# Attention scores of two heads in one matmul over all 128 rows, in a gated cross-attention and FFN kernel

## The chip, the cores and the metric

The kernel runs on one core of a Trainium2 chip. The metric is the device time of one execution in microseconds (us); lower is better. The core's engines are named as the profile names them: PE is the matmul engine (TensorE) and PEld its weight loads, DVE is VectorE, ACT is ScalarE, POOL is GpSimd, and SP is the engine from whose queue almost all transfers are issued.

## What is computed

```python
def reference(x, ctx_1024, g_xattn, g_ffn, ...):
    def xattn(q, k, v, Wq, Wk, Wv, Wo, bo):            # 16 heads of 16 dimensions
        qh = einsum('bse,hed->bhsd', q, Wq); kh = ... ; vh = ...
        scores = einsum('bhsd,bhtd->bhst', qh, kh) / sqrt(16)
        scores = where(causal, scores, -1e9)
        out = einsum('bhst,bhtd->bhsd', softmax(scores), vh)
        return concat(out) @ Wo.T + bo
    def ffn(x, ...):                                   # 256 -> 1024 -> 1024 -> 1024 -> 256
        h = silu(tlin(x, w1)) * tlin(x, w2)
        h = gelu(tlin(h, h1)); h = gelu(tlin(h, h2))
        return tlin(h, w3)                             # ternary weights, one scale per output
    x = x + tanh(g_xattn) * xattn(layernorm(x), ctx, ctx, ...)
    return x + tanh(g_ffn) * ffn(layernorm(x), ...)
```

`x` and `ctx_1024` are 64 x 128 x 256 in float32, so every one of the 64 batch rows is a sequence of 128 positions.

## The kernel before

The 64 batch rows are worked off in 32 blocks of two rows each. While the attention of block n runs, the FFN of block n-1 runs beside it, and the first steps of the attention of block n+1 are taken at the end. The order is written out by hand as one list of steps for a whole block, `ORDER` (lines 40 to 50), and one for the first block, `PROLOGUE` (lines 33 to 39). Every engine walks the same list and takes the steps that concern it, in that order; a step with a plus sign belongs to the next block. Semaphores hold an engine that comes too early. An engine's queue is strictly in order, so an instruction that waits holds all behind it.

The steps by name. On PE: `S` scores, `PV` probabilities times values, `Q`, `K`, `V` projections, `To` and `X2` transposes, `O` output projection, `L1` to `L4` the FFN layers (8 steps each for L1, L2 and L3, 4 for L4). On DVE: `s` scales and masks one group of four heads (one PSUM bank of scores), `m` its maximum and exp bias, `nh` normalises, `g` and `f` the two halves of the SiLU product of an L1 step, `b2` and `b3` sum an FFN step's two halves, `w3` takes low parts, `o` the residual and the statistics, `n2` the second layer norm, `x2` splits the transposed result into high and low parts, `y` scales the FFN's output. On ACT: `e` exponentials, `a1` the tanh of an L1 step, `h`, `a2`, `a3` copies and gelus, `to`, `x2`. On POOL: `p` splits probabilities into two fp16 parts, `nm`, `l`, `w2`, `n2`, `rx`, `z`. On SP: `D` transposes probabilities by DMA, `qw` and `kw` write the split queries and keys to DRAM, `qr.0`, `qr.1`, `kr.0`, `kr.1` bring them back for batch row 0 or 1 of the block, `lc`, `lt`, `lx`, `lr` are loads, `mv` a move and `sy` the store.

**Precision and layout of the scores.** Queries and keys are split into a high and a low part in fp32r. `place_parts` (line 340) lays them out for the score matmuls: a head's 16 dimensions times 4 combinations of parts (`COPIES = 4`, four transfers of 128 KB for each of q and k and each batch row) fill 64 partitions, so `q4` and `k4` hold two heads one above the other in the two halves of the 128 partitions.

**The scores.** `scores(n, u)` (line 921) has 4 steps per block, `S.0` to `S.3`. One step gives two groups of four heads, that is both score banks: 8 matmuls, in 4 pairs. In a pair one matmul uses the upper 64 rows and bank 0, the other the lower 64 rows and bank 1; each streams 128 key columns against 128 query columns as weights. A step waits until both banks were read by `s`. FFN matmuls use all 128 rows.

**FFN banks.** Three PSUM banks rotate over the FFN steps. `L1.3` needs the bank of `L1.0`, which is free once `f.0` is done. `L4.0` waits for the sums `b3.6` and `b3.7` (before_ffn, line 283). `L1.0` waits for `x2.1` of DVE.

Of the kernel before, what the change touches and what calls it, by code (L numbers as in the profile page):

```python
# [27 lines left out]
def steps(text):  # L28
# [5 lines left out]
    q.0 K qw Q.0 lc+ Q.1 k st v q.1 k+ W.0 kw W.1 s.0 s.1 V m.0 e.0 p.0 s.2 K+ W.2 S.0 Q.0+ m.1 lx+ p.1 qr.0 kr.0  # L34
    lt+ S.1 e.1 p.2 Q.1+ m.2 s.3 e.2 W.3 S.2 m.3 S.3 p.3 qr.1 s.4 PV.0 s.5 PV.1 m.4 PV.2 p.4 q.0+ q.1+ s.6 e.3 e.4
    kr.1 PV.3 W.4 m.5 m.6 e.5 p.5 nh.0 nm.0 s.7 W.5 D.0 D.1 kw+ nh.1 nm.1 To.0 PV.4 m.7 p.6 W.6 rx e.6 e.7 W.7 D.2
    st+ nh.2 O.0 p.7 V+ PV.5 lr PV.6 o.0 D.3 D.4 PV.7 D.5 n2.0 nm.2 to.0 nm.3 W.8 D.6 W.9 W.10 nh.3 v+ to.1 To.1 D.7
    qw+ O.1 kr.0+ F.0 F.1 o.1 x2.0 qr.0+ n2.1 s.0+ s.1+ X2.0 x2.1 rx+ p.0+ qr.1+ S.0+ X2.1 lr+ m.0+ s.2+ kr.1+ m.1+
""")
ORDER = steps("""  # L40
    lc+ S.1 L1.0 L1.1 lt+ sy L1.2 e.0 S.2 a1.0 s.3 e.1 a1.1 L1.3 h.0 L1.4 L1.5 l.0 L1.6 L1.7 a1.2 g.0 K+ a1.3 p.1
    PV.0 l.1 h.1 h.2 PV.1 L2.0 l.2 l.3 l.4 a1.4 a1.5 f.0 h.3 L2.1 g.1 f.1 h.4 l.5 l.6 g.2 l.7 a1.6 f.2 g.3 L2.2 f.3
    g.4 L2.3 f.4 L2.4 g.5 f.5 L2.5 g.6 f.6 L2.6 g.7 L2.7 h.5 a1.7 h.6 h.7 p.2 f.7 D.0 e.2 s.4 PV.2 D.1 p.3 PV.3 m.2
    m.3 m.4 b2.0 e.3 S.3 Q.0+ mv nh.0 kw+ b2.1 w2.0 L3.0 L3.1 D.2 k+ e.4 s.5 b2.2 b2.3 w2.1 w2.2 D.3 m.5 D.4 lx+
    b2.4 Q.1+ b2.5 a2.0 a2.1 a2.2 w2.3 w2.4 w2.5 L3.2 L3.3 To.0 PV.4 a2.3 b2.6 p.4 a2.4 a2.5 w2.6 PV.5 a2.6 a2.7
    L3.4 L3.5 b2.7 nm.0 s.6 s.7 O.0 w2.7 L3.6 PV.6 p.5 m.6 PV.7 V+ b3.0 To.1 L3.7 nh.1 m.7 p.6 O.1 b3.1 nm.1 e.5
    b3.2 e.6 e.7 D.5 p.7 q.0+ q.1+ a3.0 b3.3 S.0+ qw+ st+ w3.0 nm.2 to.0 X2.0 a3.1 a3.2 w3.1 a3.3 b3.4 b3.5 nh.2 o.0
    L4.0 a3.4 nh.3 D.6 L4.1 a3.5 b3.6 n2.0 nm.3 D.7 w3.2 v+ b3.7 o.1 s.0+ n2.1 kr.0+ rx+ m.0+ p.0+ w3.3 to.1 qr.0+
    a3.6 x2.0 a3.7 lr+ kr.1+ X2.1 s.1+ x2.1 m.1+ qr.1+ L4.2 z.0 L4.3 y.0 s.2+ z.1 y.1
# [1059 lines left out]
```

## Time and profile before

| | us |
|---|---|
| median of 3 runs | 1824.99 |
| lowest and highest run | 1816.38, 1828.99 |
| the profiled execution | 1814.27 |
| its span, from first to last instruction | 1812.5 |
| mean granted PE clock, share of full speed | 0.98 |
| PE busy | 1743.9 (96%) |
| DVE, ACT, POOL busy | 1383.7, 1222.9, 1081.5 |

The profile comes from one execution. The span is divided by engine and line; matmuls are pipelined, so their durations overlap, and what a matmul costs in a stream is the distance from its start to the next one's, not its own duration. The first 93 us are the prologue with the first block's attention, then 31 blocks follow that are alike, and the last stretch is the FFN of the last block alone.

### The profile page before, as it was taken

Reading aid. Unit: us, or ns where it says so; the run is one execution under the profiler, and the core shown is the slowest. Engines: PE = TensorE matmul, PEld = TensorE weight load, DVE = VectorE, ACT = ScalarE, POOL = GpSimd, SP = SyncE. Lnnn points to the kernel's source line nnn. Section 1 sums busy time; section 2 is a strip of 40 time slices with the busy share of each in tenths; the row PEclk is TensorE's granted clock in tenths of the full one; section 3 lists DMA queues with packets and bytes.
Section 4 is the critical chain, followed back from the end, with each engine's and each line's share of the span. In section 5 each row is a group of like instructions: output and inputs, shape, how many; then the busy total and the mean of one; then the engine's idle time right before and its main releaser. Section 6 shows DMA issues by size and latency. Waiting matters only on the chain.

```text
span 1812.5 us, 40485 instructions
## 1 busy us (share of the span) xinstructions
PE 1743.9 (96%) x11526; PEld 1481.4 (82%) x11526; DVE 1383.7 (76%) x3059; ACT 1222.9 (67%) x2952; POOL 1081.5 (60%) x1388
## 2 busy tenths in 40 slices
PE   4399999999999999999999999999999999999998
PEld 2288888888888888888888888888888888888876
DVE  4777887777787777787777888777788777788764
ACT  3476666677676677676767666667666667767664
POOL 2466566566656566666566665556656556665652
PEclk7599999999999999999999999999999999999999
DMA  7744545444445444454444454444454544445520
GB/s 278 227 107 121 140 127 138 112 127 115 133 136 138 114 127 115 129 142 130 120 117 126 123 139 127 132 111 127 119 136 127 140 113 126 113 133 141 126 46 8
DMA packets 395547, 231.38 MB, mean 128 GB/s; under 512 B 283136, under 2 KB 373504, under 8 KB 393984
## 3 DMA queue, kind: packets, MB, share of 16 engines
q1 hardware_dynamic: 393360, 219.23, 46.0%
q10 hardware_dynamic: 2160, 11.81, 1.8%
q8 instruction: 13, 0.21, 0.0%
q14 instruction: 14, 0.11, 0.0%
HBM read 113.53 MB, written 41.94 MB: 86 GB/s over the span
## 4 chain that ended last, share of the span: by engine, by line
PE 92%; DMA 2%; issue 2%; DVE 1%; POOL 1%; ACT 1%; SPq 0%; POOLq 0%; ACTq 0%; DVEq 0%
PE ffn L957 70%; PE work L894 13%; PE s_bank L931 4%; PE pv L948 3%; PE work L1037 2%; DMA pT<-p_parts 2%; DMA aw<-in_attn_w 0%; DVE wlow L669 0%; POOL p_parts L452 0%; SPq L348 0%; POOL p_parts L454 0%; DMA cT<-in_ctx_T 0%; ACT probs L799 0%; POOL heads L464 0%; DVE probs L594 0%
## 5 line engine op out<-in xcount | busy, mean ns | idle before, releaser
L636 DVE TENSOR_REDUCE full<-ffn 128x256 f32<-128x512 f32 x512 | 352.5, 689 | 261.1 <-PE ffn L957 259.1
L957 PE MATMUL ffn<-hb,W 128*128 128x512 f32 x2048 | 518.2, 403 | 1.0 <-POOL hb L491 1.0
L957 PE MATMUL ffn<-ha,W 128*128 128x512 f32 x2048 | 477.9, 393 | 0.6 <-POOL ha L486 0.6
L957 PEld LDWEIGHTS ffn<-ha,W 128*128 128x128 f32 x2048 | 382.1, 188 | 83.5 <-POOL ha L486 1.7
L957 PEld LDWEIGHTS ffn<-hb,W 128*128 128x128 f32 x2048 | 380.1, 188 | 79.1 <-POOL hb L491 1.6
L799 ACT ACTIVATE probs<-probs,exp_bias 128x128 f32<-128x128 f32 x1024 | 320.3, 390 | 70.7 <-DVE exp_bias L604 69.8
L454 POOL TENSOR_TENSOR p_parts<-probs,p_parts 128x512 f16<-128x512 f32 x256 | 299.5, 1170 | 20.5
L452 POOL CAST p_parts<-probs 128x512 f16<-128x512 f32 x256 | 162.3, 634 | 216.3 <-ACT probs L799 172.0
L817 ACT ACTIVATE full<-full,cols 128x256 f32<-128x256 f32 x512 | 253.8, 496 | 0.0
L957 PE MATMUL ffn<-x2T_hi,W 128*128 128x256 f32 x1024 | 252.2, 287 | 0.0
L491 POOL TENSOR_TENSOR hb<-full,hb 128x256 fp32r<-128x256 f32 x256 | 189.5, 740 | 99.6 <-ACT full L817 91.9
L957 PE MATMUL ffn<-x2T_lo,W 128*128 128x256 f32 x1024 | 245.3, 280 | 0.0
L816 ACT ACTIVATE hb<-full,cols 128x256 fp32r<-128x256 f32 x256 | 129.1, 504 | 100.6 <-DVE full L636 99.1
L957 PEld LDWEIGHTS ffn<-x2T_hi,W 128*128 128x128 f32 x1024 | 193.2, 189 | 4.4
L594 DVE SCALAR_TENSOR_TENSOR probs<-s_bank,rstd,causal 128x512 f32<-128x512 f32 x256 | 187.6, 744 | 11.7 <-PE s_bank L931 8.3
L486 POOL TENSOR_TENSOR ha<-full,ha 128x256 fp32r<-128x256 f32 x256 | 184.2, 739 | 15.5 <-ACT ha L831 12.0
L957 PEld LDWEIGHTS ffn<-x2T_lo,W 128*128 128x128 f32 x1024 | 193.3, 189 | 0.0
L840 ACT ACTIVATE full<-ffn,half_s 128x256 f32<-128x256 f32 x256 | 119.4, 466 | 84.2 <-PE ffn L957 58.9
L602 DVE TENSOR_REDUCE negmax<-probs 128x4 f32<-128x512 f32 x256 | 173.5, 678 | 0.0
L816 ACT ACTIVATE ha<-full,cols 128x256 fp32r<-128x256 f32 x256 | 128.5, 502 | 51.6 <-DVE full L636 51.2
L957 PE MATMUL ffn<-W,ha 128*128 128x256 f32 x1024 | 143.2, 288 | 1.0 <-DVE full L636 0.9
L957 PEld LDWEIGHTS ffn<-W,ha 128*128 128x128 f32 x1024 | 126.3, 189 | 7.1 <-DVE ha L642 5.7
(80 smaller groups left out, 2273.9 us busy)
## 6 DMA issues: line engine op xcount, KB each, us to landing
q<-q_saved SPq DMA_DIRECT2D x256, 128.0 KB, 2.7
k<-k_saved SPq DMA_DIRECT2D x256, 128.0 KB, 2.8
q_saved<-q_parts SPq DMA_DIRECT2D x32, 512.0 KB, 2.9
k_saved<-k_parts SPq DMA_DIRECT2D x32, 512.0 KB, 3.0
wnat<-in_ffn_w ACTq DMA_DIRECT2D x11, 1024.0 KB, 6.6
xT<-in_x_T SPq DMA_DIRECT2D x32, 256.0 KB, 2.8
cT<-in_ctx_T SPq DMA_DIRECT2D x32, 256.0 KB, 2.8
x_in<-in_x SPq DMA_DIRECT2D x32, 256.0 KB, 2.8
```

Source lines behind the costliest of these rows:

```text
L452: pool.tensor_copy(p_parts[:, t % 2, 0], probs[:, t % PSLOTS]).then_inc(p_hi_ready, 1)
L454: pool.tensor_tensor(p_parts[:, t % 2, 1], probs[:, t % PSLOTS], p_parts[:, t % 2, 0], ALU.subtract)\
L486: pool.tensor_tensor(ha_lo[:, k], full[:, k % 4], ha_hi[:, k], ALU.subtract)\
L491: pool.tensor_tensor(hb_lo[:, k], full[:, k % 4], hb_hi[:, k], ALU.subtract)\
L594: dve.scalar_tensor_tensor(probs[:, slot], s_bank[t % SBANKS][:].rearrange("p (h t) -> p h t", h=4), rstd[:, t // QROW:t // QROW + 1], cau ...
L602: dve.tensor_reduce(negmax[:, slot], probs[:, slot], AX_X, ALU.max, negate=True).then_inc(max_ready, 1)
L636: dve.tensor_reduce(full[:, m % 4], src[:].rearrange("p (a t) -> p t a", a=2), AX_X, ALU.add).then_inc(done, 1)
L799: last = act.activation(probs[:, slot, h], probs[:, slot, h], ACT.Exp, bias=exp_bias[:, slot, h:h + 1])
L816: act.activation(hi[:, m], f, ACT.Gelu, scale=scales[:, m:m + 1]).then_inc(hi_sem, 1)
L817: act.activation(f, f, ACT.Gelu, scale=scales[:, m:m + 1]).then_inc(hi_sem, 1)
L894: last = pe.matmul(dst, lhsT(kt), rhs(kt), start=kt == 0, stop=kt == KE - 1)
L957: return pe.matmul(dst, w, h, **flags)
```

## The change

The keys of a pair of heads are laid out in two blocks of columns: `k4` gets a dimension `e` of size 2, with the keys of the upper head in columns e=0 of partitions 0 to 63, those of the lower head in columns e=1 of partitions 64 to 127, and zeros elsewhere. One POOL memset at the start writes the zeros. One matmul over all 128 rows with 256 key columns then gives the scores of both heads. A score step now makes one group of four heads (one bank, two matmuls of 256 columns), so there are 8 steps per block, `S.0` to `S.7`; step t waits for the mask of group t-2. The permutation of the heads in the weights, made on the host, changes with it. `k4` takes twice the room. Each k transfer of 128 KB becomes two of 64 KB, so `kr` issues 8 transfers instead of 4; `qr` stays. Both lists of steps are new. For the stretch around the end of a block they read, per engine:

```
PE  before  L3.7 O.1 S.0+ X2.0 L4.0 L4.1 X2.1 L4.2 L4.3 | S.1 L1.0 L1.1 L1.2 S.2 L1.3 ...
PE  after   L3.7 O.1 L4.0 S.0+ L4.1 X2.0 L4.2 X2.1 L4.3 | S.1 S.2 L1.0 S.3 L1.1 L1.2 S.4 L1.3 ...
DVE before  b3.7 o.1 s.0+ n2.1 m.0+ w3.3 x2.0 s.1+ x2.1 m.1+ y.0 s.2+ y.1 | s.3 g.0 f.0 g.1 ...
DVE after   b3.7 o.1 s.0+ n2.1 w3.3 m.0+ x2.0 x2.1 y.0 s.1+ m.1+ y.1 | g.0 s.2 f.0 g.1 ...
SP  before  D.5 qw+ D.6 D.7 kr.0+ qr.0+ lr+ kr.1+ qr.1+ | lc+ lt+ sy D.0
SP  after   D.5 sy qw+ D.6 D.7 kr.0+ qr.0+ qr.1+ lr+ | kr.1 lc+ lx+ D.0
```

Elsewhere in the block, `S.5` stands after `L1.7`, `S.6` between the two `Q` steps and `S.7` between `L3.0` and `L3.1`; `q.0+` and `q.1+` of DVE stand before `b3.1` instead of after `b3.2`.

```diff
-        k4 = sb("k4", [P, ROWS, QROW, KE, P], F32R)
+        k4 = sb("k4", [P, ROWS, QROW, 2, KE, P], F32R)
...
+                if kind == "kr" and isinstance(n, int) and n == 0 and row == 0:
+                    sp.wait_ge(keys_cleared, 1)
...
                 for copy in range(COPIES):
-                    part = copy % 2 if kind == "qr" else copy // 2
-                    sp.dma_start(dst[copy:P:COPIES, row].rearrange("p j m t -> p j (m t)").bitcast(F32),
-                                 saved[:, part, row].rearrange("(p j) x -> p j x", j=QROW))\
-                        .then_inc(q_placed[row] if kind == "qr" else k_placed[row], 16)
+                    if kind == "qr":
+                        sp.dma_start(q4[copy:P:COPIES, row].rearrange("p j m t -> p j (m t)").bitcast(F32),
+                                     q_saved[:, copy % 2, row].rearrange("(p j) x -> p j x", j=QROW))\
+                            .then_inc(q_placed[row], 16)
+                    else:
+                        for e in range(2):
+                            sp.dma_start(k4[e * HALF + copy:(e + 1) * HALF:COPIES, row, :, e]
+                                         .rearrange("p j m t -> p j (m t)").bitcast(F32),
+                                         k_saved[e * HALF:(e + 1) * HALF, copy // 2, row]
+                                         .rearrange("(p j) x -> p j x", j=QROW)).then_inc(k_placed[row], 16)
...
             pool.memset(vs[:], 1.0).then_inc(pool_const, 1)
+            pool.memset(k4[:].bitcast(F32), 0.0).then_inc(keys_cleared, 1)
...
-            def scores(n, u):
-
-                row = u // 2
-                wait(pe, masked_ready, n * NQ + 2 * u)
-                if u % 2 == 0:
+            def scores(n, t):
+
+                row, j = t // QROW, t % QROW
+                wait(pe, masked_ready, n * NQ + t - 1)
+                if j == 0:
                     wait(pe, q_placed[row], 16 * COPIES * (n + 1))
-                    wait(pe, k_placed[row], 16 * COPIES * (n + 1))
-                for i in range(4):
-                    j, m = u % 2 * 2 + i // 2, i % 2
-                    for e in range(2):
-                        last = pe.matmul(s_bank[e][:, i * P:(i + 1) * P], q4[e * HALF:(e + 1) * HALF, row, j, m],
-                                         k4[e * HALF:(e + 1) * HALF, row, j, m], start=True, stop=True)
-                        if i == 3:
-                            last.then_inc(scores_ready[e], 1)
+                    wait(pe, k_placed[row], 16 * COPIES * 2 * (n + 1))
+                for m in range(KE):
+                    last = pe.matmul(s_bank[t % SBANKS][:, m * TOK:(m + 1) * TOK].rearrange("p (e t) -> p e t", e=2),
+                                     q4[:, row, j, m], k4[:, row, j, :, m], start=True, stop=True)
+                last.then_inc(scores_ready[t % SBANKS], 1)
```

## Rows read from the trace of the kernel before

**Rows 1.** The page, chain of work that ended last, by line.
```profile
PE ffn L957 70%; PE work L894 13%; PE s_bank L931 4%; PE pv L948 3%; PE work L1037 2%; DMA pT<-p_parts 2%; DMA aw<-in_attn_w 0%; DVE wlow L669 0%; POOL p_parts L452 0%; SPq L348 0%; POOL p_parts L454 0%; DMA cT<-in_ctx_T 0%; ACT probs L799 0%; POOL heads L464 0%; DVE probs L594 0%
```
**Rows 2.** Busy time by stretch: one block, and part of the prologue.
```profile
950.88:1004.78 53.90, 53.90 (x361) 45.97 (x360) 42.24 (x96) 37.66 (x92) 33.36 (x44) 1.00 0.48 126
...
20.00:40.00 20.00, 9.46 (x32) 6.20 (x32) 11.00 (x12) 7.51 (x9) 4.15 (x3) 0.62 0.89 294
```
**Rows 3.** PE in order of time around one score step: start us, us, what.
```profile
959.05 0.28 PE L957 MATMUL ffn<-x2T_hi,W 128*128 128x256 f32 x1
...
959.64 0.28 PE L957 MATMUL ffn<-x2T_lo,W 128*128 128x256 f32 x1
959.85 0.66 PE L931 MATMUL s_bank<-k,q 64*128 64x128 f32 x8
960.44 0.39 PE L957 MATMUL ffn<-x2T_hi,W 128*128 128x256 f32 x1
960.66 0.28 PE L957 MATMUL ffn<-x2T_lo,W 128*128 128x256 f32 x1
```
**Rows 4.** Groups of PE by shape, the scores: xcount | busy us, mean ns.
```profile
L931 PE MATMUL s_bank<-k,q 64*128 64x128 f32 x1024 | 87.0, 290 | 12.7 <-DVE probs L594 9.6 <-DMA k<-k_saved 2.8 <-DMA q<-q_saved 0.2
```
**Rows 5.** PE in order of time over the end of a block.
```profile
946.05 1.97 PE L894 MATMUL work<-aw,cT 128*128 128x256 f32 x8
947.86 0.38 PE L1037 MATMUL work<-ident,heads 128*128 128x128 f32 x2
...
949.93 1.02 PE L894 MATMUL work<-aw,oT 128*128 128x256 f32 x4
950.88 0.66 PE L931 MATMUL s_bank<-k,q 64*128 64x128 f32 x8
...
951.67 2.13 PE L957 MATMUL ffn<-W,ha 128*128 128x256 f32 x16
...
953.94 2.36 PE L957 MATMUL ffn<-W,ha 128*128 128x256 f32 x16
956.23 0.66 PE L931 MATMUL s_bank<-k,q 64*128 64x128 f32 x8
956.82 0.39 PE L957 MATMUL ffn<-x2T_hi,W 128*128 128x256 f32 x1
```
**Rows 6.** Waits of PE's weight loads, 174 to 1700 us: us in total, times, longest.
```profile
PEld ffn L957 <- DVE ha L642: 5.5, 28, 0.2
```
**Rows 7.** DVE in order of time over the same end of a block.
```profile
950.19 0.69 DVE L636 TENSOR_REDUCE full<-ffn 128x256 f32<-128x512 f32 x1 [0.16 <-PE ffn L957]
...
954.36 0.69 DVE L642 TENSOR_TENSOR ha<-full,ha 128x512 fp32r<-128x512 f32 x1
...
955.30 0.74 DVE L594 SCALAR_TENSOR_TENSOR probs<-s_bank,rstd,causal 128x512 f32<-128x512 f32 x1
955.96 0.41 DVE L732 TENSOR_TENSOR x2T_lo<-work,x2T_hi 128x256 fp32r<-128x256 f32 x1
...
959.53 0.48 DVE L629 SCALAR_TENSOR_TENSOR full<-ffn,half_s,full 128x256 f32<-128x256 f32 x1
```
**Rows 8.** SP in order of time over the end of a block (issuing instructions).
```profile
938.55 0.34 SPq L336 DMA_DIRECT2D q_saved<-q_parts  x1
...
942.53 2.48 SPq L348 DMA_DIRECT2D k<-k_saved  x4
945.26 2.45 SPq L348 DMA_DIRECT2D q<-q_saved  x4
951.71 0.42 SPq L322 DMA_DIRECT2D xres<-in_x  x1
```
**Rows 9.** The issues of q and k: duration ns min/median/max; then time to landing.
```profile
L348 SPq DMA_DIRECT2D k<-k_saved x8: 516/594/603, 942.5 to 954.2; - x8
...
DMA to landing us min/median/max: 2.6/2.7/2.9
```
**Rows 10.** POOL groups, 0 to 20 us: xcount | busy us, mean ns.
```profile
L435 POOL MEMSET vs<- 128x1568 bf16 x1 | 1.4, 1406 | 0.0
```

More of the change, by code:

```diff
@@ L33 @@
 PROLOGUE = steps("""
[L34 to L38, printed above, removed]
+    q.0 k kw qw q.1 st lx+ K W.0 W.1 e.0 W.2 Q.0 Q.1 s.0 e.1 m.0 p.0 V p.1 kr.0 W.3 S.0 s.1 qr.0 s.2 m.1 p.2 m.2 v
@@ L39 @@
+    e.2 lr kr.1 S.1 qr.1 S.2 s.3 s.4 W.4 S.3 p.3 p.4 lc+ K+ S.4 Q.0+ lt+ D.0 k+ PV.0 m.3 S.5 Q.1+ e.3 S.6 PV.1 W.5
+    PV.2 nh.0 p.5 m.4 s.5 nm.0 D.1 D.2 rx S.7 e.4 D.3 nm.1 p.6 m.5 e.5 kw+ s.6 W.6 PV.3 p.7 s.7 nm.2 To.0 O.0 q.0+
+    m.6 nh.1 m.7 e.6 W.7 D.4 e.7 q.1+ D.5 D.6 V+ to.0 D.7 W.8 qw+ o.0 PV.4 nh.2 st+ nm.3 W.9 W.10 nh.3 PV.5 kr.0+
+    PV.6 PV.7 To.1 v+ O.1 to.1 F.0 n2.0 o.1 X2.0 x2.0 S.0+ n2.1 F.1 qr.0+ qr.1+ s.0+ m.0+ x2.1 p.0+ s.1+ X2.1 lr+
+    m.1+ rx+
 """)
 ORDER = steps("""
-    lc+ S.1 L1.0 L1.1 lt+ sy L1.2 e.0 S.2 a1.0 s.3 e.1 a1.1 L1.3 h.0 L1.4 L1.5 l.0 L1.6 L1.7 a1.2 g.0 K+ a1.3 p.1
@@ L42 @@
[L42 to L46, printed above, removed]
@@ L47 @@
-    b3.2 e.6 e.7 D.5 p.7 q.0+ q.1+ a3.0 b3.3 S.0+ qw+ st+ w3.0 nm.2 to.0 X2.0 a3.1 a3.2 w3.1 a3.3 b3.4 b3.5 nh.2 o.0
-    L4.0 a3.4 nh.3 D.6 L4.1 a3.5 b3.6 n2.0 nm.3 D.7 w3.2 v+ b3.7 o.1 s.0+ n2.1 kr.0+ rx+ m.0+ p.0+ w3.3 to.1 qr.0+
-    a3.6 x2.0 a3.7 lr+ kr.1+ X2.1 s.1+ x2.1 m.1+ qr.1+ L4.2 z.0 L4.3 y.0 s.2+ z.1 y.1
+    S.1 g.0 kr.1 s.2 S.2 f.0 l.0 e.0 L1.0 a1.0 g.1 e.1 lc+ lx+ S.3 L1.1 L1.2 a1.1 S.4 L1.3 L1.4 D.0 L1.5 L1.6 p.1
+    l.1 l.2 lt+ h.0 l.3 L1.7 a1.2 l.4 f.1 h.1 S.5 a1.3 g.2 l.5 h.2 f.2 K+ a1.4 PV.0 h.3 g.3 PV.1 l.6 L2.0 L2.1 L2.2
@@ new lines @@
+    L2.3 L2.4 L2.5 f.3 a1.5 g.4 L2.6 f.4 s.3 l.7 D.1 D.2 p.2 nm.0 w2.0 h.4 g.5 a1.6 f.5 g.6 L2.7 f.6 h.5 a1.7 g.7
+    f.7 m.2 kw+ Q.0+ S.6 mv D.3 Q.1+ PV.2 PV.3 m.3 L3.0 h.6 h.7 e.2 e.3 S.7 p.3 s.4 L3.1 L3.2 L3.3 b2.0 D.4 D.5 nh.0
+    a2.0 To.0 p.4 PV.4 b2.1 m.4 w2.1 k+ w2.2 sy b2.2 b2.3 s.5 e.4 a2.1 qw+ PV.5 w2.3 a2.2 a2.3 L3.4 L3.5 w2.4 w2.5
+    D.6 b2.4 m.5 a2.4 a2.5 b2.5 b2.6 a2.6 a2.7 b2.7 O.0 s.6 w2.6 w2.7 m.6 p.5 e.5 s.7 b3.0 m.7 L3.6 nh.1 PV.6 q.0+
+    D.7 nm.1 p.6 kr.0+ e.6 PV.7 qr.0+ q.1+ b3.1 b3.2 p.7 nh.2 V+ st+ e.7 w3.0 a3.0 b3.3 nm.2 b3.4 w3.1 to.0 To.1
@@ L50 @@
+    a3.1 a3.2 b3.5 a3.3 o.0 L3.7 O.1 qr.1+ L4.0 nh.3 b3.6 a3.4 n2.0 w3.2 a3.5 nm.3 v+ b3.7 o.1 lr+ s.0+ n2.1 to.1
+    w3.3 rx+ m.0+ a3.6 a3.7 x2.0 x2.1 S.0+ L4.1 y.0 X2.0 s.1+ z.0 p.0+ L4.2 X2.1 m.1+ y.1 L4.3 z.1
 """)
@@ L182, in program @@
         pool_const = sem("pool_const")
+        keys_cleared = sem("keys_cleared")
         gates_ready = sem("gates_ready")
@@ L334, in write_parts @@
                 for placed in q_placed if kind == "qw" else k_placed:
-                    hold(placed, 16 * COPIES * n)
+                    hold(placed, 16 * COPIES * (1 if kind == "qw" else 2) * n)
                 sp.dma_start(saved.rearrange("p a r x -> p (a r x)"),
@@ L340, in place_parts @@
             def place_parts(n, kind, row):
-                saved, dst = (q_saved, q4) if kind == "qr" else (k_saved, k4)
+                if kind == "kr" and isinstance(n, int) and n == 0 and row == 0:
+                    sp.wait_ge(keys_cleared, 1)
                 hold(q_written if kind == "qr" else k_written, 16 * n + 16)
@@ L1076 @@
     from concourse.bass_utils import run_bass_kernel_spmd
-    nc = bacc.Bacc("TRN2", target_bir_lowering=False, num_devices=1)
+    nc = bacc.Bacc("TRN2", target_bir_lowering=False, num_devices=1, dynamic_dma_scratch_size=8192)
     def kt_rows(w):
@@ L1084 @@
     b, s, e = ctx.shape
-    heads = [inputs[f"L0_xattn_{w}"].reshape(2, 2, 2, 2, e, -1).transpose(4, 3, 1, 5, 0, 2).reshape(e, e)
+    heads = [inputs[f"L0_xattn_{w}"].reshape(4, 2, 2, e, -1).transpose(3, 1, 2, 4, 0).reshape(e, e)
              for w in ("Wq", "Wk")] + [inputs["L0_xattn_Wv"].transpose(1, 0, 2).reshape(e, e)]
```

## The prediction

> **What bounds the kernel.** I read the chain of work that ended last first: it lies almost wholly on PE, 70% on the FFN matmuls and 4% on the scores [rows 1]. Then I cut out one block: in 53.90 us PE is busy for 53.90, DVE for 42.24, ACT for 37.66 and POOL for 33.36, at full clock [rows 2]. So the length of a block is the sum of PE's start-to-start distances, and about 0.2 us of it is a wait that I come to below. What counts is how many ns of PE's stream a score step takes, and whether PE in the new order still finds everything ready. DVE has 11.7 us of slack in a block, but not everywhere: around a block's end PE waits for single results of DVE.
>
> **What a score step costs now.** The FFN stream there runs at one 256-column matmul per 0.118 us (959.05 to 959.64, five of them) [rows 3]. The step's first matmul starts 0.21 us after the last FFN matmul, its eight take 0.59 us until the FFN starts again, and the FFN's first one then takes 0.22 us instead of 0.118. From 959.64 to 960.66 that is 1.02 us, of which two FFN matmuls would take 0.236: the step costs **0.79 us**. The eight matmuls last 290 ns each on average [rows 4] and are over in 0.66 us, so they overlap in pairs. The excess at the way in (0.09) and out (0.10) shows that going from full rows to half rows and back is not free; the rest of 0.59 beyond four regular slots is a slow first pair.
>
> **What it costs after.** Two steps replace one: four fp32r matmuls of 128 rows and 256 columns, the very shape of the FFN's first layer. The nearest row gives 0.118 each [rows 3], so 0.47 us for two steps. Bounds: no less than 0.118, as I see no faster 256-column matmul here; above, the fp32 projections of 256 columns take 1.81 us for eight, 0.226 each [rows 5] (946.05 to 947.86), which would make 0.90. I take 0.118, since data type, rows and columns are those of the FFN. Saved: 0.79 - 0.47 = **0.32 us per old step, 1.28 per block**.
>
> The rule that speaks against the change stands in the Trainium skill, "TensorEngine Tiling (Array Packing)", section "When to Use Tiling": for a contraction of 64 rows or less, split the array into row tiles, for up to twice the speed. The trace agrees that the pairs overlap. By that rule the new form, with 1024 columns one after another where there were 512, takes twice the time of the pairs. The row speaks otherwise, as 256 columns take 0.118 us. The same page, "Key Properties", says that a change of tiling mode drains the engine, and the 0.09 and 0.10 agree with it.
>
> **The end of the block, part by part.** I call E the end of `O.1`, 950.79 (949.93 plus four slots of 0.216, an estimate; the score step starts 0.09 later) [rows 5].
> - *L4.3 and w3.3.* The second pair of L4 steps lasts 2.36 us against 2.13 for the first [rows 5], and the waits say why: 5.5 us in 28 blocks for the low parts `w3` [rows 6], **0.20 per block**. In the new order L4.3 is reached about 0.5 us earlier (scores before it cost 0.24 instead of 0.79), but `w3.3` stands ahead of `m.0` and comes about 0.8 earlier than its 954.36 [rows 7]. The wait goes.
> - *L4.0* now follows `O.1` at once and needs `b3.7`, which ends at 950.88 [rows 7], 0.09 after E, plus a semaphore. New wait **0.12 per block**.
> - *L1.0.* Before, everything from E to the end of L4.3 takes 956.14 - 950.79 = 5.35 us; less 0.79 and 0.23 it is 4.33, and with three new steps (0.71) and the 0.12 PE reaches L1.0 at 955.95. It needs `x2.1`, which began at 955.96 and before which a mask of 0.66 stood (955.30) [rows 7]; that mask is moved behind, so it begins near 955.30 and ends at 955.71. No wait, with 0.2 to spare. L1.0 comes 0.87 earlier than its 956.82.
> - *L1.3.* From `x2.1` to `f.0` DVE has the same pieces as before in another order (one maximum, two masks, two `y`, `g.0`, `f.0`): `f.0` ends 4.05 us after `x2.1` begins (955.96 to 960.01) [rows 7], so at 959.35. PE needs 3 x 0.94 for three L1 steps and 0.47 for two score steps, and is there at 959.25. Before, a score step of 0.79 gave cover. New wait **0.15**, and as much for the steps behind it, where DVE takes 0.9 per step and PE 0.94: **0.3 together**.
> - *SP.* `kr` issues 8 transfers instead of 4, and `kr.1` is moved behind `qr.1` and `lr`, into the next block. Four k issues take 2.48 us [rows 8], 0.64 apart; the first of a group takes 516 ns, the median 594 [rows 9]. What one of half the size takes no row shows. Bounds: half, 0.32, if it goes by size; 0.64, if it doesn't. The rows lean to the latter: 512 KB are issued in 0.34 and 256 KB in 0.42 [rows 8], both less than these 128 KB. I take 0.55, the first one's 516 ns and a gap. Then `kr.0` takes 4.4 us instead of 2.6. `D.7` ahead of it comes about 0.6 earlier in the new order, because `q.1+` is no longer behind `b3.2` (an estimate from the order). So `kr.0` starts at 941.9, `qr.0` is issued by 948.9 and has landed by 951.0; S.0 comes at 951.84 (E + 0.12 + 0.93). Covered. `qr.1` is issued by 951.5, `lr` (x1 is ready at 951.6) by 952.2, then the loop's end (0.3) and eight k until 956.9; the last lands 2.7 us after its start [rows 9], 959.1. S.4 is wanted at 955.95 + 2.83 + 0.24 = 959.0. Wait **0.1**, and it overlaps with L1.3's. At 0.64 per issue it is 1.4 us later: wait 1.5. At 0.32 none. Behind `kr.1` queue `lc`, `lx` and the first transpose `D.0`, which PE wants only 7 us later, at PV.0.
> - *The rest* of the steps (S.5, S.6, S.7) needs masks that DVE has finished microseconds before; nothing on the way.
>
> **Prologue.** The memset of `k4` writes 4096 floats per partition; 1568 bf16 take 1.4 us [rows 10], so some 3.7 us, done before the keys come at about 25 us. Eight k issues ahead of the first scores cost about 2 us where PE is half idle (9.46 of 20) [rows 2]. I count +2, bounds -2 and +5.
>
> **The sum.** Per block: 1.28 + 0.20 - 0.12 - 0.3 - 0.1 = 0.96. Times 31 blocks: 29.8; less 2: **28 us**. Against the profiled execution, 1814.3, that is 1786. The median of the runs, 1825, lies 10.7 above it; I take the gain from there, as the result is a median too: **1797 us**, a ratio of 0.985.
>
> **Rivals.**
> 1. *The keys of row 1 come late.* If a half-size issue costs as much as a whole one, S.4 waits 1.5 us per block and hides the 0.4 of the L1 waits. 1.28 + 0.20 - 0.12 - 1.5 = about -0.14 per block: 4 us lost, 6 with the prologue, 1831; with half of it, gain 12, 1813. For it: size did not set issue time in the other rows. Against it: the issues after the first are 80 ns longer, so something fills up with 128 KB that 64 KB would fill less. Chance 0.23, nearly all within 1%.
> 2. *No new waits.* 1.48 x 31 = 46 less 0 to 2: 1780. Chance 0.07.
> 3. *Slower: a 256-column score matmul runs at the projections' 0.226.* Two steps then cost 0.90 against 0.79: 0.11 x 4 = 0.44 lost, 0.52 in waits, 0.20 won, 0.76 per block, 24 us and 2: 1851. It decides from 0.2 us per matmul on (gain then nil before waits). For it: only that no such matmul with two column blocks is in the trace. Against it: the FFN's stream. Chance 0.04.
> 4. *Slower by SP alone*: rival 1 with `D.7` not earlier, so that S.0 waits 0.5 too and S.4 2.1: 0.9 per block lost, 1855. Chance 0.03.
>
> My forecast, a gain of 18 to 40 us (1785 to 1807), has 0.63.
>
> **Range and chances.** About 1% is what a measurement of this kernel can tell from no change. Faster by over 1% are the forecast and rival 2: 0.70. Within 1%: rival 1, 0.23. Slower: 3 and 4, 0.07. The range for 8 in 10 goes from 1775 to 1822: rival 2 in, the milder half of rival 1 in, the rest out.
>
> **What would show it.** A score step's two matmuls 0.12 apart and the FFN before and after at 0.118, without the 0.21 and 0.22; a block of 52.9 us; no wait of L4 for `w3`; small waits of PE for `b3.7` and for `f.0`. A k issue at about 0.5 us, 8 per row. PE waiting for the k transfer in every block would mean rival 1, score matmuls 0.2 apart rival 3. If the block is 52.9 and the time is not down, the prologue has it.

## The result and the profile after

| | before | after |
|---|---|---|
| median us | 1824.99 (5 runs) | 1857.31 (5 runs) |
| lowest and highest | 1815.95, 1828.99 | 1854.32, 1868.90 |
| the profiled execution's span | 1812.5 | 1867.1 |
| PE busy | 1743.9 | 1730.6 |
| a block in the middle of the run | 53.90 | 54.92 |

The ratio of after to before is **1.0215, 95% interval 1.018 to 1.0249**: the change makes the kernel 32 us slower. The forecast was 28 us faster. The profiled execution of after is the slowest of its five.

The page of after, the chain of work that ended last, by engine and by line (before it lay almost wholly on PE [rows 1]):

```profile
PE 56%; SPq 29%; issue 6%; DMA 6%; DVE 1%; POOL 1%; ACT 0%; POOLq 0%; DVEq 0%
PE ffn L964 45%; SPq L356 15%; SPq L351 8%; PE work L904 6%; SPq L366 4%; DMA k<-k_saved 4%; DMA pT<-p_parts 2%; PE s_bank L939 2%; PE pv L955 2%; SPq L324 1%; SPq L309 0%; PE work L1044 0%; DMA aw<-in_attn_w 0%; DVE full L639 0%; DVE full L632 0%
```

SP's queue now holds 29% of it, line 356 (the issue of k) alone 15%. One block of after, from one `L1.0` to the next, as busy time of PE, PEld, DVE, ACT and POOL:

```profile
939.26:994.18 54.92, 52.98 (x344) 45.57 (x343) 42.12 (x95) 40.51 (x95) 32.90 (x44) 1.00 0.46 124
```

PE is busy 0.92 us less per block than before, 52.98 for 53.90 [rows 2], so the matmuls did get cheaper. But PE now stands idle for 1.94 us of the block, where before it had none. Its waits in the 28 blocks between 174 and 1750 us (total, times, longest) say for what:

```profile
PEld s_bank L939 <- DMA k<-k_saved: 41.8, 28, 2.1
...
PE s_bank L939 <- DMA k<-k_saved: 36.1, 28, 1.9
...
PE s_bank L939 <- DMA q<-q_saved: 6.3, 24, 0.7
PE ffn L964 <- DVE full L646: 5.0, 28, 0.2
```

36.1 us for k in 28 blocks is 1.3 per block, q 0.2, `b3.7` 0.2. In order of time, over the end of a block (start, us, what; the stretch that answers to [rows 5]):

```profile
987.52 1.02 PE L904 MATMUL work<-aw,oT 128*128 128x256 f32 x4
988.72 1.20 PE L964 MATMUL ffn<-W,ha 128*128 128x256 f32 x8 [0.18 <-DVE full L646]
990.13 0.50 PE L939 MATMUL s_bank<-k,q 128*128 128x256 f32 x2 [0.20 <-DMA q<-q_saved]
990.46 1.10 PE L964 MATMUL ffn<-W,ha 128*128 128x256 f32 x8
...
993.72 0.63 PE L939 MATMUL s_bank<-k,q 128*128 128x256 f32 x4
994.18 0.28 PE L964 MATMUL ffn<-x2T_hi,W 128*128 128x256 f32 x1
...
995.12 0.43 PE L939 MATMUL s_bank<-k,q 128*128 128x256 f32 x2
995.39 0.28 PE L964 MATMUL ffn<-x2T_hi,W 128*128 128x256 f32 x1
...
997.24 0.28 PE L964 MATMUL ffn<-x2T_lo,W 128*128 128x256 f32 x1
998.75 0.51 PE L939 MATMUL s_bank<-k,q 128*128 128x256 f32 x2 [1.23 <-DMA k<-k_saved]
999.09 0.28 PE L964 MATMUL ffn<-x2T_hi,W 128*128 128x256 f32 x1
```

Three things are to be seen. `S.1` and `S.2` take 0.46 us for four matmuls (993.72 to 994.18): 0.115 each, where 0.118 was forecast. `S.4` begins at 998.75, 1.51 us after the matmul ahead of it, in place of 0.12. And a step that has waited starts slowly: `S.4` takes 0.34 to the next matmul where `S.3` (995.12 to 995.39) takes 0.27 and the regular pace is 0.24. Why `S.4` waits is in the chain of the same stretch, followed back from it (start, us, what):

```profile
...
992.09 0.57 SPq L356
992.66 0.06 issue
992.72 0.58 SPq L356
...
995.89 0.59 SPq L356
996.48 0.04 issue
996.52 2.18 DMA k<-k_saved
998.70 0.04 issue
998.75 0.51 PE s_bank L939 x2
```

In it stand eight k transfers, 0.63 us from start to start, and the last one's way to memory. Ahead of them SP has issued, in order of time (`kr.0`; `qr.0` and `qr.1`; `lr`; `kr.1`):

```profile
980.05 5.02 SPq L356 DMA_DIRECT2D k<-k_saved  x8
985.42 5.19 SPq L351 DMA_DIRECT2D q<-q_saved  x8
990.78 0.46 SPq L324 DMA_DIRECT2D xres<-in_x  x1
992.09 5.03 SPq L356 DMA_DIRECT2D k<-k_saved  x8
```

The issues of k in the middle of the run (ns min/median/max), with their landing:

```profile
L356 SPq DMA_DIRECT2D k<-k_saved x293: 561/594/602, 499.4 to 1492.9; - x147
...
DMA to landing us min/median/max: 2.1/2.3/2.9
```

A transfer of 64 KB costs SP 594 ns, and one of 128 KB cost it 594 as well [rows 9]. Only the landing is 0.4 us earlier. One part of the change is not named in the text ahead: the line that makes the program object also sets `dynamic_dma_scratch_size=8192`. It is not what makes the issues dear, for x2_before_split_k leaves it out and its k transfers of 64 KB take 593 ns (median).

### The profile page after: what moved, and what is told of

It is laid out like the page before. It is cut to its first block, busy times and chain, and to the rows that moved or that the text cites. A ratio compares the mean times of both kernels' runs of the same rounds, so it can differ in the third digit from the quotient of the medians.

```text
span 1867.1 us, 39954 instructions
## 1 busy us (share of the span) xinstructions
PE 1730.6 (93%) x11014; PEld 1482.3 (79%) x11014; DVE 1389.0 (74%) x3059; ACT 1319.2 (71%) x3014; POOL 1075.4 (58%) x1389
## 2 busy tenths in 40 slices
DMA packets 399643, 231.39 MB, mean 124 GB/s; under 512 B 287232, under 2 KB 377600, under 8 KB 398080
## 4 chain that ended last, share of the span: by engine, by line
PE 56%; SPq 29%; issue 6%; DMA 6%; DVE 1%; POOL 1%; ACT 0%; POOLq 0%; DVEq 0%
PE ffn L964 45%; SPq L356 15%; SPq L351 8%; PE work L904 6%; SPq L366 4%; DMA k<-k_saved 4%; DMA pT<-p_parts 2%; PE s_bank L939 2%; PE pv L955 2%; SPq L324 1%; SPq L309 0%; PE work L1044 0%; DMA aw<-in_attn_w 0%; DVE full L639 0%; DVE full L632 0%
## 5 line engine op out<-in xcount | busy, mean ns | idle before, releaser
L964 PE MATMUL ffn<-hb,W 128*128 128x512 f32 x2048 | 510.5, 399 | 1.2 <-POOL hb L501 1.2
L646 DVE TENSOR_REDUCE full<-ffn 128x256 f32<-128x512 f32 x512 | 346.2, 686 | 136.7 <-PE ffn L964 107.3
L964 PEld LDWEIGHTS ffn<-hb,W 128*128 128x128 f32 x2048 | 375.6, 188 | 77.0 <-POOL hb L501 2.1
L462 POOL CAST p_parts<-probs 128x512 f16<-128x512 f32 x256 | 157.2, 614 | 207.4 <-ACT probs L809 165.0
L604 DVE SCALAR_TENSOR_TENSOR probs<-s_bank,rstd,causal 128x512 f32<-128x512 f32 x256 | 191.4, 748 | 97.4 <-PE s_bank L939 96.9
L964 PE MATMUL ffn<-x2T_lo,W 128*128 128x256 f32 x1024 | 251.4, 283 | 0.0
L939 PE MATMUL s_bank<-k,q 128*128 128x256 f32 x512 | 113.9, 315 | 64.5 <-DMA k<-k_saved 39.7
```

The lines of the kernel that those rows point to most:

```text
L462: pool.tensor_copy(p_parts[:, t % 2, 0], probs[:, t % PSLOTS]).then_inc(p_hi_ready, 1)
L604: dve.scalar_tensor_tensor(probs[:, slot], s_bank[t % SBANKS][:].rearrange("p (h t) -> p h t", h=4), rstd[:, t // QROW:t // QROW + 1], cau ...
L646: dve.tensor_reduce(full[:, m % 4], src[:].rearrange("p (a t) -> p t a", a=2), AX_X, ALU.add).then_inc(done, 1)
L964: return pe.matmul(dst, w, h, **flags)
```

## The experiments

Nine kernels and the changed one again. Each ratio is to runs of the kernel before that were taken beside that kernel, so it is not quite the quotient with 1824.99. "Block" is the median distance from one `L1.0` to the next over the profiled execution's 31 blocks, worked out from the trace.

| kernel | median us | ratio to before, 95% | block |
|---|---|---|---|
| before | 1824.99 | | 53.90 |
| after | 1857.31 | 1.0215 (1.018 to 1.0249) | 54.92 |
| x1_half_k | 1820.16 | 0.9998 (0.9974 to 1.0022) | 53.98 |
| x3_before_full_rows | 1803.09 | 0.9882 (0.9859 to 0.9905) | 53.44 |
| x2_before_split_k | 1904.44, one run | | 56.88 |
| m5_few_after | 1814.81 | 0.9954 (0.9932 to 0.9976) | 54.00 |
| y1_rx_moved | 1796.81 | 0.9872 (0.9853 to 0.9890) | 53.35 |
| m6_few_before_order | 1819.64 | 0.9993 (0.9973 to 1.0014) | 53.45 |
| y3_own_order | 1813.82 | 0.9968 (0.9945 to 0.9990) | 53.44 |
| z2_s0_first | 1789.58 | 0.9818 (0.9780 to 0.9855) | 53.08 |
| z4_s4_late | 1788.87 | 0.9814 (0.9777 to 0.9851) | 53.09 |
| a2_after_again | 1858.69, one run | | 54.96 |

### The changed kernel with half of its k transfers

```diff
-                        for e in range(2):
+                        for e in range(1):
```

> The changed kernel without the k transfers into the lower 64 partitions (e=1), so four issues of 64 KB per batch row instead of eight; the scores of the lower heads are left out by this, since their keys stay zero. Everything else, the order too, is as in the changed kernel. Theory A (SP: an issue of 64 KB costs SP as much as one of 128 KB, 0.63 us, so the k transfers of row 1 come late for S.4 and the q transfers of row 0 a little late for S.0): both waits go, each with the 0.1 us that PE needs to get going again; a block of 54.9 us becomes about 53.0, and the time about 1857 - 31 x 1.9 = 1798 us. Theory B (the new order: masks and f.0 of DVE would hold S.4 and L1.3 anyway, and the k transfers only come last among several that are late): the block stays above 54.4, the time above 1840. Theory C (the prologue holds most of the loss): the block hardly moves and the first FFN matmul comes some 10 us earlier.

Measured: 1820.16, 37 us less than after. The waits for k and q are gone, so the eight issues per row in place of four are where these 37 us went. (The bytes of k are halved as well; m5_few_after below, in which the waits go too although more bytes are moved, speaks for the number of issues.) But the kernel is no faster than before, although its score matmuls are the cheap ones. The waits of PE that remain (28 blocks):

```profile
PEld ffn L964 <- DVE x2T_lo L742: 13.3, 28, 0.7
...
PE ffn L964 <- DVE x2T_lo L742: 7.4, 27, 0.5
PE ffn L964 <- DVE full L646: 5.0, 28, 0.2
PE ffn L964 <- DVE y L714: 3.2, 16, 0.3
```

`L1.0` now waits for `x2.1`, which it did not in after. So each theory held a part (53.98 lies between their 53.0 and 54.4): SP costs 37 us, and behind it stands a second bound, DVE at the block's end, that takes most of the rest. Why `x2.1` is late is seen in the same stretch of DVE, and of POOL:

```profile
807.67 0.95 DVE L614 TENSOR_SCALAR exp_bias<-negmax 128x4 f32<-128x4 f32 x1
808.54 0.74 DVE L742 TENSOR_TENSOR x2T_lo<-work,x2T_hi 128x256 fp32r<-128x256 f32 x2
```
```profile
807.31 1.29 POOL L453 TENSOR_TENSOR xres<-xres,bo_tg 128x512 f32<-128x512 f32 x1 [1.63 <-DMA xres<-in_x]
```

An instruction over four elements per partition takes 0.95 us, and ends (808.62) when POOL's `rx` ends (808.60). In after it takes 0.17: SP issues `lr` so late there that `rx` starts only at 993.84, when `m.0` is over (993.30). This gave the theory that was tested with y1 below.

### Full-row scores in the order of before

The kernel before, its steps where they were, with each `S` step made of four full-row matmuls, and four k transfers of 64 KB per row. Like x1_half_k it leaves out the scores of the lower heads.

```diff
-                for i in range(4):
-                    j, m = u % 2 * 2 + i // 2, i % 2
-                    for e in range(2):
-                        last = pe.matmul(s_bank[e][:, i * P:(i + 1) * P], q4[e * HALF:(e + 1) * HALF, row, j, m],
-                                         k4[e * HALF:(e + 1) * HALF, row, j, m], start=True, stop=True)
+                for t in (2 * u, 2 * u + 1):
+                    j = t % QROW
+                    for m in range(KE):
+                        last = pe.matmul(s_bank[t % SBANKS][:, m * TOK:(m + 1) * TOK].rearrange("p (e t) -> p e t", e=2),
+                                         q4[:, row, j, m], k4[:, row, j, :, m], start=True, stop=True)
```

> The kernel before with its old order and its four score steps, but the scores as matmuls over all 128 rows with 256 key columns (four matmuls per step instead of eight); k4 in two column blocks, cleared at the start, and only the four k transfers of 64 KB into the upper 64 partitions per batch row (the scores of the lower heads are left out by this). It measures what the matmuls alone bring. Theory A: a step costs 0.47 us instead of 0.79, a block 53.9 - 1.28 = 52.6, less what DVE cannot follow (0.2): 52.6 to 52.9, the time 1785 to 1794 us. Theory B (PE is not what sets the block around the scores; DVE's results come no earlier): 53.5 or more, 1813 or more.

Measured: 1803.09, 1.2% faster than before, between what the two theories expected: of the 1.28 us that PE saves in a block, 0.46 reach the block's length. PE over the block's end:

```profile
790.95 2.13 PE L966 MATMUL ffn<-W,ha 128*128 128x256 f32 x16
793.31 0.41 PE L1046 MATMUL work<-ident,x2n 128*128 128x128 f32 x2 [0.23 <-DVE x2n L736]
```

`X2.1` comes earlier than DVE's `n2.1` and waits 0.23, and the wait for `w3.3` stays (PEld ffn for DVE ha, 5.4 us in 28 blocks). From `o.1` (790.62) on DVE runs here with no pause longer than 0.2 us. Where PE was ahead of this chain by less than what it saves, the saving turns into a wait.

### The kernel before with its k transfers split

Each k transfer of 128 KB as two of 64 KB, nothing else.

```diff
-                    sp.dma_start(dst[copy:P:COPIES, row] ...
+                        for e in range(2):
+                            sp.dma_start(k4[e * HALF + copy:(e + 1) * HALF:COPIES, row] ...
```

> The kernel before, its old scores and order, but each k transfer of 128 KB made as two of 64 KB (upper and lower half of the partitions), so eight k issues per batch row. The same bytes are moved and the same is computed. Theory A (cost per issue): 2.5 us more on SP per row; the q transfers of row 0 land at about 952.3 instead of 949.8 where S.0 stands at 950.9, a wait of 1.4; the idle time of SP ahead of lr takes up the first 2.5, row 1 lands 2.5 later, S.2 waits about 0.9; a block of 56.2, 1895 us. Theory S (cost by size, and the k transfers of the changed kernel are slow for another reason, their strided place in k4): 53.9, 1820 us.

Measured: 1904.44, the block 56.88: eight more issues, of the same bytes, cost 80 us with no other edit. `S.0` waits in every block, and in some the next row's first step as well (28 blocks; total, times, longest):

```profile
PE s_bank L936 <- DMA q<-q_saved: 63.0, 40, 2.9
```

Not all of the 80 us is SP's. After the wait of `S.0` the granted clock of PE often falls for 3.4 us to 0.50, the lower of its two levels (1.2 and 2.4 GHz), as here (start, us, what; then the stretch with its PEclk):

```profile
1001.94 1.00 PE L936 MATMUL s_bank<-k,q 64*128 64x128 f32 x8 [1.85 <-DMA q<-q_saved]
...
1002.10:1005.50 3.40, 3.40 (x21) 3.28 (x22) 2.37 (x3) 1.18 (x3) 1.37 (x2) 0.50 0.52 153
```

17 of the 31 blocks hold such a stretch and take 57.84 (median); the 14 at full clock take 55.34, 1.44 more than before. The 31 blocks together are 85 us longer. By an estimate from these medians the late transfers account for some 45 of them (31 times 1.44) and the stretches at the lower clock for some 40 (17 times 2.5). In after only three of the 31 blocks hold such a stretch.

So the split needs neither the new matmuls nor the new order to cost something, but it does not account for all that after loses. If the 1.28 of the cheaper matmuls reached the block whole, 55.34 would become 54.06, where after has 54.92. So up to 0.9, an estimate, may belong to the new order, in which `L4.0` follows `O.1` at once and `kr.1` stands behind `qr.1` and `lr`; no run with the split and the new matmuls in the old order was made.

### The whole change with few, large transfers

The changed kernel, complete, in which q and k are each written to DRAM in two copies (6 transfers per block in place of 2), so that one transfer of 512 KB brings a row's q and two of 256 KB its k: 3 issues per row in place of 12.

```diff
-                for copy in range(COPIES):
-                    if kind == "qr":
-                        sp.dma_start(q4[copy:P:COPIES, row] ...
+                if kind == "qr":
+                    sp.dma_start(q4[:, row].rearrange("p j m t -> p (j m t)").bitcast(F32),
+                                 q_saved[:, :, row].rearrange("d a (p j) x -> p (d a) (j x)", j=QROW))
```

> The changed kernel in its own order, with the placing made of few transfers: the queries are written to DRAM twice (two transfers) and the keys twice (four), each copy in its place, so that one transfer of 512 KB fetches q and two of 256 KB fetch k per batch row, three issues where there were twelve. Everything is computed. Theory A: SP is free early, all waits for q and k go, block 53.0 or less, time 1790 to 1800 us. Theory B (the order): above 54.4 us a block. If the transfers themselves are slow (contention, few engines), q or k would be waited for in spite of few issues.

Measured: 1814.81, 42.5 us less than after. An issue costs no more for eight times the bytes (ns min/median/max), at the price of a later landing. The kernel moves 264.92 MB in all, after 231.39:

```profile
L358 SPq DMA_DIRECT2D q<-q_saved x38: 531/533/535, 511.9 to 1484.7; - x38
...
DMA to landing us min/median/max: 4.3/4.8/5.8
```

But 1790 to 1800 was missed: the waits of PE are those of x1_half_k, for `x2.1`, `y.1` and `b3.7`. SP is no longer the bound, the block's end on DVE is.

### POOL's `rx` out of the end of the block

m5_few_after with POOL's `rx` (1.29 us, for the next block's residual) moved from behind `w3.3` to behind `p.4`. It then runs in the block that needs it and no longer at the end of the one before.

```diff
-    w3.3 rx+ m.0+ a3.6 a3.7 ...
+    w3.3 m.0+ a3.6 a3.7 ...
-    a2.0 To.0 p.4 PV.4 ...
+    a2.0 To.0 p.4 rx PV.4 ...
```

> The kernel with few q and k transfers and the changed order (m5), with one step moved: rx, POOL's addition of the bias to the residual (1.3 us), from the end of a block, where in m5 and in x1 the tiny exp_bias instruction of m.0 on DVE lasts 0.6 to 0.95 us instead of 0.17 and ends with that POOL instruction, to the middle of the next block, behind p.4. Theory L (DVE's exp_bias waits for the POOL instruction, x2.0 and x2.1 behind it come late and PE waits for x2.1 ahead of L1.0): exp_bias of m.0 takes 0.17, PE's wait at L1.0 of 0.4 to 0.7 goes, the block goes from 54.0 to 53.5, the time from 1815 to about 1800 us. Theory O (the waits at L1.0 come from the order of DVE's own work, the mask of S.0 being late): exp_bias may be short, but the block stays at 53.8 to 54.0.

Measured: **1796.81**, 18 us less than with `rx` where it was, and faster than before by 1.3%. The same instruction of DVE, and what follows it:

```profile
783.53 0.17 DVE L620 TENSOR_SCALAR exp_bias<-negmax 128x4 f32<-128x4 f32 x1
783.61 0.74 DVE L748 TENSOR_TENSOR x2T_lo<-work,x2T_hi 128x256 fp32r<-128x256 f32 x2
```

The waits for `x2.1` and `y` are gone; `b3.7` (5.1 us in 29 blocks) and the mask `s.2` ahead of `S.4` (5.2 in 28) are left. The trace shows it elsewhere too: of 226 such instructions in the steady blocks of before, 57 take over 0.25 us in place of 0.17, 15 us too much in all; in x1 and m5 it is 108 each, 43 us; in y1 still 56, 24 us, at places where PE does not wait for it. All of them end with an instruction of POOL, most with one of two operands, some 24 of the 108 with a cast. The Trainium skill, "SBUF — State Buffer", section "Who interferes with whom", says that an instruction of VectorE in a mode that uses two ports, and one of GpSimd, each hold a shared pair of ports for the whole instruction while the other is blocked, and names tensor_scalar among those that can enter such a mode. The 0.95 us that end with POOL's instruction agree; that it is this pair of ports no run here shows.

### The order of before, complete

m6_few_before_order is x3_before_full_rows with all keys, brought by few transfers. y3_own_order is that with 8 steps, `S.1` ahead of `X2.1`, `w3.3` ahead of `m.0`, `s.2` put off to the next block, `s.3` behind `f.4` and `rx` behind `p.3`, so several moves at once.

```diff
-    L4.0 a3.4 nh.3 D.6 L4.1 a3.5 b3.6 n2.0 nm.3 D.7 w3.2 v+ b3.7 o.1 s.0+ n2.1 kr.0+ rx+ m.0+ p.0+ w3.3 ...
+    L4.0 a3.4 nh.3 D.6 L4.1 S.1+ a3.5 b3.6 n2.0 nm.3 D.7 w3.2 v+ b3.7 o.1 s.0+ n2.1 kr.0+ w3.3 m.0+ p.0+ ...
```

> The old order and four score steps of the kernel before, full-row score matmuls, and the few q and k transfers (three issues per batch row). Everything is computed. It is x3 with nothing left out. Theory P (the cheaper matmuls bring 0.5 us per block in the old order, and SP is no limit with few issues): 53.4 us per block, 1803 us, as x3. If the larger transfers (landing 3.8 to 4.7 us instead of 2.3 to 2.7) come late for S.0, PE waits for q or k there and the block is 53.9 or more.

> m6 with eight score steps and the old order changed where x3 showed PE waiting: S.1 of the next block stands ahead of X2.1 (PE waited 0.23 there for x2n), w3.3 ahead of m.0 on DVE (L4.3 waited 0.27 with its restart), s.3 is put off until f.4, S.2 to S.5 single, and rx is moved to the middle of the block as in y1. Theory D (from o.1 to f.0 DVE works without a pause, 7.7 us, and sets when L1.3 can start; taking one mask of 0.66 out of that stretch shortens the block by what the waits of PE allow, 0.4 to 0.5): 52.9 to 53.1 us per block, 1788 to 1793 us. Theory N (the waits only move to L1.4 and on): 53.4, 1803 us, as x3.

Measured: the block of m6 is 53.45, as expected, so the missing keys of x3 gave it nothing. But the time, 1819.64, is 17 us over the expectation. The 31 blocks together take the same as in x3 (1657.6 and 1657.5 us); the first `L1.0` comes at 108.1 us (99.1 in x3, 92.8 before), so what the profiles show of the difference sits ahead of it. y3's block is 53.44, not 52.9 to 53.1: the wait for `w3.3` went, one for `x2.1` took its place (0.26 us at `L1.0`), and `X2.1` waits no less than in x3. In the old order, these moves only moved the wait.

### `S.0` ahead of `L4.0`, and `S.4` later

z2_s0_first is y1_rx_moved with `S.0` of the next block right behind `O.1`; z4_s4_late is z2 with `S.4` behind `L1.3` and its mask behind `f.0`.

```diff
-    L3.7 O.1 qr.1+ L4.0 nh.3 b3.6 ... x2.0 x2.1 S.0+ L4.1 y.0
+    L3.7 O.1 S.0+ qr.1+ L4.0 nh.3 b3.6 ... x2.0 x2.1 L4.1 y.0
```
```diff
-    S.1 g.0 kr.1 s.2 S.2 f.0 l.0 ... a1.1 S.4 L1.3 L1.4
+    S.1 g.0 kr.1 S.2 f.0 s.2 l.0 ... a1.1 L1.3 S.4 L1.4
```

> y1_rx_moved with one step moved: S.0 of the next block stands right behind O.1, ahead of L4.0, as in the kernel before. Theory Q (what PE waits for at a block's end is DVE's last sum b3.7, and any ready matmul put ahead of L4.0 hides it): the wait of L4.0, 0.33 us and 0.1 of slower first matmuls behind it, goes, since S.0's two matmuls (0.24 us) cover 0.24 of it; 0.25 to 0.35 us per block, the block 53.35 -> 53.0 to 53.1, the time about 1787 us (8 to 11 us less). Rival R (DVE's chain behind b3.7 bounds the stretch, and PE only waits elsewhere): the wait comes back at L1.0 for x2.1 or at L1.3 for f.0, the block stays 53.3 to 53.4 and the time 1797.

> z2_s0_first with S.4 one L1 step later (behind L1.3 instead of ahead of it) and on DVE the mask s.2 behind f.0 instead of ahead of it. Theory Q: S.4 waits 0.3 to 0.44 us for the mask s.2 in y1_rx_moved; with s.2 behind f.0 it would wait as long, but it now stands 0.94 us later, and f.0, on which L1.3 hangs, comes 0.7 earlier: another 0.3 to 0.4 us per block, the block about 52.7, the time 1775 to 1780. Rival R (DVE bounds the stretch): nothing, the time as that of z2_s0_first within 3 us.

Measured, z2: **1789.58**, 1.8% faster than before, the block 53.08, as theory Q had it. PE in y1 and then in z2:

```profile
778.40 1.02 PE L910 MATMUL work<-aw,oT 128*128 128x256 f32 x4
779.61 1.19 PE L970 MATMUL ffn<-W,ha 128*128 128x256 f32 x8 [0.18 <-DVE full L652]
780.63 0.39 PE L945 MATMUL s_bank<-k,q 128*128 128x256 f32 x2
```
```profile
775.89 1.02 PE L910 MATMUL work<-aw,oT 128*128 128x256 f32 x4
776.56 0.58 PE L945 MATMUL s_bank<-k,q 128*128 128x256 f32 x2
777.09 2.10 PE L970 MATMUL ffn<-W,ha 128*128 128x256 f32 x16
```

`L4.0` starts 1.21 us after `O.1` starts in y1 and 1.20 in z2, with `S.0` in between: it fits into the wait and is free. z4 gained nothing, 1788.87, as rival R had it. The wait of `S.4` for its mask is gone,

```profile
732.38 0.40 PE L945 MATMUL s_bank<-k,q 128*128 128x256 f32 x2
732.87 0.39 PE L970 MATMUL ffn<-x2T_hi,W 128*128 128x256 f32 x1
733.10 0.28 PE L970 MATMUL ffn<-x2T_lo,W 128*128 128x256 f32 x1
```

but `L1.4` behind it waits for DVE's `f` (0.49 us from `S.4` to it in place of 0.24, and 0.23 in place of 0.12 for its first matmul). Here DVE's chain sets the pace, and this later place of `S.4` on PE does not help.

### The changed kernel again

> The changed kernel itself once more. The first L1 step of the first block began at 110.5 us in its first profile, and at 90 to 108 us in the profiles of the others. If that comes from the kernel's code, it begins at 110 again, within 2 us; if it comes from how fast the first loads arrive in an execution, it lies elsewhere between 90 and 110, while the median block stays 54.9 us.

Measured: the first `L1.0` at 102.5 us, with 110.5 in the first profile of the same kernel; the median block 54.96. So it is not the kernel's code alone: the prologue's length varies by at least 8 us between executions of one kernel. The landing of the weights' eleven transfers of 1 MB varies as well, here of after and of after again (median us to landing in the last column):

```profile
wnat<-in_ffn_w ACTq DMA_DIRECT2D x11, 1024.0 KB, 11.7
```
```profile
wnat<-in_ffn_w ACTq DMA_DIRECT2D x11, 1024.0 KB, 10.0
```

In x1 (first `L1.0` at 108.4) it is 13.4 us, in before 6.6. But 8.1 goes with a first `L1.0` at 108.1 in m6 and at 90.9 in z2, and 6.6 with 89.9 in y1 and 96.1 in y3. So late landings go with late starts here, but do not account for all of them. What makes the prologue long was not tried and stays open.

## Why the prediction was wrong

**The sum, per block.** Predicted in the first column, in us won (+) or lost (-); in the second what the traces of before and after show.

| term | predicted | measured |
|---|---|---|
| score steps | +1.28 | +1.28 |
| wait for `w3.3` | +0.20 | +0.20 |
| `L4.0` waits for `b3.7` | -0.12 | -0.44 |
| `S.0` waits for q | 0 | -0.47 |
| `S.4` waits for k | -0.1 | -1.5 |
| `L1.3` and behind it | -0.3 | about -0.1 |
| sum | +0.96 | -1.03 |

The median block grew by 1.02 us, and the 31 blocks together by 36.6 (1670.0 to 1706.6; three of them hold stretches at a granted clock of 0.50 and are 1.6 to 2.9 longer than the median). The median time grew by 32.3. In the two profiled executions the first `L1.0` also comes 17.7 us later (110.5 for 92.8), but these are a slow one of after and a quick one of before. a2_after_again, at 1858.69 close to after's median, has it at 102.5, and by an estimate an execution of before at its median of 1825 has it at some 103.5 (92.8 and the 10.7 that the profiled one is quicker). So the loss in the medians is that of the blocks.

**Right: the price of the matmuls.** Four of 256 columns over all rows take 0.47 us where eight on half the rows took 0.79 [rows 3]. The distances of 0.21 ahead of them and 0.22 behind them are 0.12 now. Rival 3 is out. The Trainium skill's rule to split the array for 64 rows or less ("TensorEngine Tiling (Array Packing)", "When to Use Tiling") would have had the step grow; here it shrank, and x3_before_full_rows, which has the new matmuls in the old order, is 1.2% faster.

**Right: `w3.3`.** The wait for it is no longer among PE's waits.

**Wrong, and decisive: SP's queue.** The terms that failed are the wait of `S.4` for k, put at 0.1 and measured at 1.5, and that of `S.0` for q, put at nothing ("Covered") and measured at 0.47. The step behind both is the time on SP. The prediction named both bounds of an issue, 0.32 and 0.64, saw that the rows leaned to the latter, and took 0.55. It is 0.59 and 0.04 to the next, 0.63: "the first one's 516 ns and a gap" held only for the first of a group.

`kr.0` begins 8.33 us before `O.1` ends (980.05 against 988.38, which is 987.52 and four slots of 0.216), not 8.9, since `D.7` came only a little earlier. `kr.0` and `qr.0` take 7.85, not 7.0. So the last q of row 0 starts at 987.30 and lands at about 990.0, where PE wants it at 989.8; `S.0` starts at 990.13, and 0.1 slower: the -0.47. `kr.1` begins 3.71 after `O.1`, not 1.7, and its last transfer lands 10.3 after `O.1` (998.70) in place of 8.3. PE, itself held 0.8 by the two waits before, wants it at 8.98. That is the 1.4, and the slow start makes it 1.5.

The 2.0 us by which the last k is late are made up of four things. The 16 issues of k, each 0.08 dearer, give 1.2. The pauses between the groups, 0.35 between `kr.0` and `qr.0` (rows 8 had shown 0.25 and the sum had none), and `lr` with the loop's end, 1.4 for 1.0, give 0.8. `D.7` gives 0.6. The landing after 2.2 us in place of 2.7 takes 0.5 back. So the choice of 0.55 between the bounds is the largest piece, but not the whole.

With 0.64, the prediction's own rival 1, the sum would have been near nothing; with the 0.5 of rival 4 beside it, it would have come out on the right side. The measured waits, 0.47 and 1.5, lie between the two rivals: rival 4 had 0.5 and 2.1. That 1.5 is also what rival 1 says is in part luck, for it counted neither the pauses and `D.7` nor the earlier landing and PE's own lateness, which nearly cancel. The chances given were 0.23 for rival 1 and 0.03 for rival 4. Two of their sums do not come out of their terms: half of rival 1's wait gives a gain of some 17 and not 12, and rival 4's waits give 1.24 lost per block, 1865 and not 1855, so that its closeness to 1857 says little.

x1_half_k confirms the cause (37 us back with eight issues per block gone), and x2_before_split_k that the split alone, with the matmuls and the order of before, makes the q transfers late. How the loss divides between the dearer queue and the place of `kr.1` in the new order no run tells apart.

**Wrong: `L4.0`.** `b3.7` ends 0.96 us after `O.1` begins, just as before. But PE starts 0.24 after that end (988.48 to 988.72), not 0.03, and its first matmuls are 0.1 slower. The prediction put the path from one engine's end to another's start at almost nothing. z2_s0_first shows the wait to be real and avoidable: 0.27 of the block and 7 us.

**Right only by another's lateness: `L1.0`.** No wait was predicted, with 0.2 to spare, and none is seen in after. But the sum on DVE left out POOL's `rx`, which holds DVE's small instruction when the two meet. In after they do not meet, because SP issues `lr` late and `rx` comes behind `m.0`. In x1_half_k and m5_few_after, where SP has more room, they do, and `L1.0` waits 0.4 us (median) and is 0.1 slower in starting; with `rx` away, in y1, the wait is gone. Even with SP free, the forecast of 1797 was met only by this further edit.

**The chances.** Faster by over 1% had 0.70, and the price of an issue, on which it hung, had been left to one choice between two bounds. 1857 lies above the range, which left rival 4 out.

## What to carry to other kernels

An issued transfer of k or q cost its queue about the same at 64, 128 and 512 KB, so count a change's transfers, not its bytes, and where rows of other sizes lean to one bound, take that bound. When a strict queue is nearly full over a stretch, add up everything on it up to the last thing that is waited for, pauses between groups included: 0.08 us per issue became 1.2 in the block, and the pauses, with `lr`, 0.8 more. A wait can cost more than its length: look at the granted clock behind it. What an engine saves reaches the time only as far as the others are ahead of it: fill the wait that appears with a step that is ready, and look whether an instruction of POOL holds a small one of DVE.
